# A DLRM tower on one core: hot ids laid out once per partition, a later load of the other ids, and another order of work

## The chip, the cores and the metric

The kernel runs on one core of one Trainium2 chip. The metric is the device time of one execution in microseconds (us); lower is better. PE is TensorE, DVE is VectorE, ACT is ScalarE, POOL is GpSimd, SP is SyncE, which only issues DMAs here.

## The reference

```python
e = jnp.stack([tbl_0[ids[:, 0]], ..., tbl_31[ids[:, 31]]], axis=1)     # 512 x 32 x 64, f32
idx_i, idx_j = np.triu_indices(32, k=1)                                # 496 pairs of fields
left = jnp.einsum('bpd,pde->bpe', e[:, idx_i, :], W)                   # W: 496 x 64 x 64
z = jnp.sum(left * e[:, idx_j, :], axis=-1)                            # 512 x 496
h = jnp.concatenate([z, dense_ctx], axis=1)                            # 512 x 512
h = jnp.maximum(h @ W_top1 + b_top1, 0.0)                              # 512 wide
h = jnp.maximum(h @ W_top2 + b_top2, 0.0)                              # 256 wide
y = h @ W_top3                                                         # 512 x 1
```

The tables have 1,000 to 125,000 rows of 64 numbers. Everything is f32.

## The kernel before, in words

The batch of 512 is worked in four quarters of 128 rows, one row per partition. The 32 fields form 16 units of two fields. The 496 pairs form 31 groups of 16; a group is named by the units it moves (`moving(g)`, the left factors) and the units it multiplies with (`others(g)`). Group 0 holds the pairs inside units. W stays in SBUF, one 256 KB load for each group, and serves all four quarters.

For each quarter and group:
- PE multiplies the transposed embeddings `xt` with W into one of three PSUM slots (`LEFT_BUFS`), 1024 columns wide;
- DVE multiplies the slot with the other factor (a product);
- the product is summed over 64 numbers in one of four ways, the last letter of the word in `ORDER`: A by ACT (`add_rows`, 16 accumulating instructions, a ring of four buffers), D by a DVE reduction (`sum_rows`), P by POOL (`add_halves`, six halvings, a ring of two buffers), C by PE (the group is computed transposed, `col_group`, and summed by matmuls with a selector, `reduce`).

A, D and P read the other factor from the gathered rows, C from their transpose.

The rows come in two ways. The 24 large or middle tables, and all fields in quarters 1 to 3, are gathered by 120 indirect DMAs of POOL (`fetch`, L396), one for each field and quarter. Eight small tables ("hot", units 12 to 15) are, for the first quarter only, loaded whole by SP (8 loads of 256 KB, `load_hot`, L336), and looked up by matmul: DVE compares the ids with row numbers (`compare`, L515, 16 instructions in two sets), PE multiplies the tables with these 0/1 matrices (`look_up`, L675, words `h0` and `h1`). For that the ids of the four fields of a set must stand in every partition: `load_ids` (L342) reads one row of 4 x 128 ids from DRAM to all 128 partitions.

Gathered units are transposed by PE and copied to `xt` by ACT or DVE (`turn`, a word like `0t6-9a`: quarter 0, units 6 to 9, the copy by ACT where it ends in `a`).

The order of all this is written out by hand as words in `ORDER` (L51): `0g8` is a gather of unit 8 in quarter 0, `o0.1` a half set of compares, `0:21A` the matmul and product of group 21, `0=21` its sum, `f`, `z` the folding of the sums into z, `l1.0`, `m1`, `n1` the three dense layers of a span of columns. Each engine walks the list and does what is its own, strictly in that order, and waits on semaphores for the rest. All the engines' orders follow from this one list, and so does the order of the W loads (`W_ORDER`, the order of quarter 0's groups).

SP's queue (L346 on): ids of quarter 0, hot ids of set 0, four tables, hot ids of set 1, W loads number 0 and 1, four tables, the ids of the three later quarters (L355), then W loads 2 to 30. Loads 2 to 7 go in pairs, each pair behind the landing of a unit that quarter 0 gathers: the first two to be complete in `GATHERED` and so on (L358). From number 8 (`W_AHEAD`) a load waits for the product of the group eight places before it. POOL waits for the later ids only before its first gather of quarter 1 (L421).

Of the kernel before, what the change touches and what calls it, by code (L numbers as in the profile page):

```python
# [211 lines left out]
def build(nc, a):  # L212
    ctx = ExitStack()
    with ctx:
# [118 lines left out]
        def _(sp):  # L333
# [8 lines left out]
            def load_ids(d):  # L342
                sp.dma_start(hot_ids[d], a["hot_ids"][4 * d:4 * d + 4, :].unsqueeze(0).to_broadcast([P, 4, PB])
                             ).then_inc(hot_ids_loaded[d], 16)
# [4 lines left out]
            for d in range(1, HOT_SETS):  # L349
                load_ids(d)  # L350
                load_w(W_ORDER[d - 1])
                if d == HOT_SETS - 1:
                    load_w(W_ORDER[d])
# [565 lines left out]
```

## Time and profile before

| | us |
|---|---|
| median of 3 runs | 200.62 (200.47 to 201.2) |
| the profiled execution | 200.62 |
| its span (first to last instruction) | 198.5 |
| outside the span | 2.12 |
| DVE / ACT / PE / POOL busy | 181.4 / 173.5 / 190.0 / 144.5 |
| granted TensorE clock | 1.0 in every slice |

A busy PE is not PE at its peak: matmuls are pipelined, and their ends are modelled. Instructions of DVE overlap a little, too, so the cost of one in a row of many is the distance from start to start, not its duration. A row of the timeline gives the start, the time until the last of the merged instructions ends, the engine, line, operation and tiles, the count, and in brackets the idle time before it with what ended it.

### The profile page before, as it was taken

To read this page: it belongs to the slowest core of one execution; us is meant where nothing else is said; L and a number is where in the kernel's file an instruction comes from. 1 tells how busy PE (TensorE), PEld (TensorE's weight loads), DVE (VectorE), ACT (ScalarE), POOL (GpSimd) and SP (SyncE) were. 2 spreads that over 40 slices of the span, in tenths; PEclk is the share of its full clock that TensorE was granted. 3 is DMA by queue.
4 is the path that set the end of the run, shared out by engine and by line. 5 is a ranking of instruction groups with operands and counts; after the bars stand their busy time and mean duration, and the time that the engine had idled before them with its cause. 6 is when DMAs were issued, how large, how long until landed. Compare 5 with 4: busy or idle time off the path is not lost.

```text
span 198.5 us, 7004 instructions
## 1 busy us (share of the span) xinstructions
PE 190.0 (96%) x2340; PEld 155.3 (78%) x2340; DVE 181.4 (91%) x196; ACT 173.5 (87%) x1587; POOL 144.5 (73%) x181
## 2 busy tenths in 40 slices
PE   6968899999999999999999999999999999999994
PEld 6856778789678777978778877987866789868983
DVE  2663999999999999999999999999999999999952
ACT  6001999999999998999999999999999999999920
POOL 5787777777777777777777777777787885898620
PEclk9999999999999999999999999999999999999999
DMA  3996778887481111111111111111110100000000
GB/s 96 362 346 215 201 184 253 252 253 227 116 314 26 31 25 28 28 30 28 30 26 31 28 26 31 26 31 26 29 22 16 27 3 3 0 5 2 3 0 0
DMA packets 11099, 16.80 MB, mean 85 GB/s; under 512 B 3624, under 2 KB 3624, under 8 KB 10936
## 3 DMA queue, kind: packets, MB, share of 16 engines
q1 hardware_dynamic: 7224, 12.43, 19.1%
q0 software_dynamic: 3840, 3.94, 10.1%
q8 instruction: 18, 0.29, 0.7%
q14 instruction: 17, 0.14, 0.3%
HBM read 16.36 MB, written 0.00 MB: 82 GB/s over the span
## 4 chain that ended last, share of the span: by engine, by line
PE 49%; ACT 16%; DVE 16%; issue 9%; DMA 4%; POOL 4%; DVEq 0%; ACTq 0%
PE left L714 21%; ACT prod_act L442 15%; PE left L724 9%; PE zsum L737 6%; DVE prod_act L566 5%; DVE prod_col L586 4%; POOL rows L396 4%; PE left L797 4%; DMA rows<-tbl_dram,ids 3%; DVE prod_dve L566 2%; PE left L787 2%; PE left L703 2%; DVE sums L611 2%; PE zsum L745 2%; PE left L692 1%
## 5 line engine op out<-in xcount | busy, mean ns | idle before, releaser
L442 ACT ACTIVATE prod_act<-prod_act 128x64 f32<-128x64 f32 x784 | 162.8, 602 | 0.3 <-DVE prod_act L566 0.3
L442 ACT ACTIVATION_READ_ACCUMULATOR prod_act<-prod_act 128x1 f32 x784 | 161.1, 515 | 0.0
L396 POOL DMA_INDIRECT rows<-tbl_dram,ids x120 | 114.6, 955 | 37.7 <-issue 34.3
L714 PE MATMUL left<-w,xt 64*128 64x256 f32 x584 | 73.5, 387 | 1.0 <-DVE prod_col L586 0.7
L714 PEld LDWEIGHTS left<-w,xt 64*128 64x128 f32 x584 | 52.4, 187 | 14.2 <-issue 5.4
L566 DVE TENSOR_TENSOR prod_act<-left,rows 128x1024 f32<-128x1024 f32 x45 | 53.8, 1215 | 1.6 <-DMA rows<-tbl_dram,ids 1.4
L724 PEld LDWEIGHTS left<-xt,w 64*128 64x128 f32 x752 | 45.2, 188 | 4.3 <-issue 2.1
L724 PE MATMUL left<-xt,w 64*128 64x128 f32 x752 | 48.2, 276 | 0.0
L586 DVE TENSOR_TENSOR prod_col<-left,xt 128x1024 f32<-128x1024 f32 x39 | 46.1, 1214 | 0.2 <-PE left L724 0.2
L409 POOL TENSOR_TENSOR prod_pool<-prod_pool 128x512 f32<-128x512 f32 (+4 forms) x45 | 27.4, 609 | 6.4 <-DVE prod_pool L566 3.5
L737 PE MATMUL zsum<-prod_col,selector 128*32 128x256 f32 x376 | 25.0, 385 | 0.1
L566 DVE TENSOR_TENSOR prod_dve<-left,rows 128x1024 f32<-128x1024 f32 x19 | 23.0, 1216 | 0.3 <-PE left L714 0.2
L611 DVE TENSOR_REDUCE sums<-prod_dve 128x16 f32<-128x1024 f32 x19 | 22.9, 1207 | 0.0
L737 PEld LDWEIGHTS zsum<-prod_col,selector 128*32 128x32 f32 x376 | 9.9, 109 | 9.7 <-issue 2.3
L479 ACT ACTIVATE xt<-left 128x1024 f32<-128x1024 f32 (+3 forms) x8 | 8.6, 1076 | 8.3 <-PE left L692 8.3
L787 PE MATMUL left<-z,w 128*128 128x256 f32 (+1 forms) x64 | 11.8, 335 | 0.0
L787 PEld LDWEIGHTS left<-z,w 128*128 128x128 f32 x64 | 9.8, 190 | 1.9 <-DVE prod_dve L566 0.7
L566 DVE TENSOR_TENSOR prod_pool<-left,rows 128x1024 f32<-128x1024 f32 x9 | 10.9, 1213 | 0.0
L515 DVE TENSOR_SCALAR prod_col<-prod_act,row_cast 128x512 f32<-128x512 int32 x16 | 6.8, 496 | 3.7 <-DMA prod_act<-hot_ids_dram 3.7
L583 DVE TENSOR_TENSOR prod_col<-left,xt 128x1024 f32<-128x1024 f32 x8 | 9.7, 1216 | 0.1
L675 PE MATMUL left<-prod_col,w 128*64 128x128 f32 x96 | 5.9, 277 | 2.2 <-DMA w<-tbl_dram 2.2
L703 PE MATMUL left<-w,xt 64*128 64x64 f32 x128 | 7.7, 271 | 0.0
(48 smaller groups left out, 100.1 us busy)
## 6 DMA issues: line engine op xcount, KB each, us to landing
w<-pair_w_dram SPq DMA_DIRECT2D x31, 256.0 KB, 3.4
rows<-tbl_dram,ids POOLq DMA_INDIRECT x120, 2.5
w<-tbl_dram SPq DMA_DIRECT2D x6, 256.0 KB, 4.9
w<-w_top_dram SPq DMA_DIRECT2D x1, 1024.0 KB
prod_act<-hot_ids_dram SPq DMA_DIRECT2D x2, 256.0 KB, 5.3
h<-tbl_dram SPq DMA_DIRECT2D x2, 256.0 KB, 7.0
w<-w_top_dram SPq DMA_DIRECT2D x1, 512.0 KB
z<-dense_t_dram SPq DMA_DIRECT2D x16, 2.0 KB
```

The source lines that it names most:

```text
L396: pool.indirect_dma_start(out=rows[:, part % ROW_BUFS, n, h, :], out_offset=None, in_=a[f"tbl_{f}"], in_offset=bass.IndirectOffsetOnAxis(a ...
L409: pool.tensor_tensor(prod[:, :, :half], prod[:, :, :half], prod[:, :, half:2 * half], ALU.add).then_inc(pool_halved, 1)
L442: op = act.activation(p, p, ACT.Copy, accum_out=act_sums[:, k:k + 1])
L566: dve.tensor_tensor(out.rearrange("p (j e) d -> p j (e d)", j=4), slot(item).rearrange("p (j e) -> p j e", j=4), other.unsqueeze(1).to_bro ...
L583: dve.tensor_tensor(out, slot(item).rearrange("p (h u b) -> p h u b", h=2, b=PB), other, ALU.mult).then_inc(dve_taken, 1)
L586: dve.tensor_tensor(out.rearrange("p h (j m) b -> p (h j) (m b)", j=2), slot(item).rearrange("p (j e) -> p j e", j=4), other, ALU.mult).th ...
L611: dve.tensor_reduce(sums_of(part, g), prod.rearrange("p (h u o) d -> p h u o d", h=2, o=2), AXIS.X, ALU.add).then_inc(dve_summed, 1)
L703: mm = pe.matmul(slot(item)[:, col:col + D], xt[own, part % 2, 2 * k + half, :], w[own, INSIDE, :, :].rearrange("p u c -> p (u c)")[:, D * ...
L714: mm = pe.matmul(slot(item)[:, col:col + P * per], xt[own, part % 2, GROUPS[g][i][0], :], w[own, g, i:i + per, :], start=True, stop=True)
L724: mm = pe.matmul(slot(item)[:, col:col + PB], w[own, g, i, :], xt[own, part % 2, n, :], start=True, stop=True)
L737: mm = pe.matmul(zsums(pair)[32 * s:32 * s + 32, :], selector[:, 30 - 2 * q:62 - 2 * q], prod_col[:, (COL_FROM + c) % COL_BUFS, half, odd: ...
L787: mm = pe.matmul(slot(item)[:, :n], w1[:, c, P * k:P * k + P], z[:, c, SPANS[i]], start=(c == 0), stop=(c == NZ - 1))
```

## The change

It has four parts.
- The hot ids stand in DRAM as 2 x 128 x 4 x 128 numbers, each partition's copy in its own 2 KB; `load_ids` reads them straight instead of one row 128 times.
- In SP's queue W load 1 comes after the second four tables instead of before them, and the later quarters' ids are loaded behind W loads 0 to 7 instead of ahead of W load 2.
- `ORDER` and `ACT_GROUPS` are new. Sums by way and quarter: A 12, 12, 14, 11 become 11, 12, 12, 12; C 15, 16, 9, 7 become 16, 16, 13, 3; D 4, 3, 7, 5 become 4, 3, 6, 7; P 0, 0, 1, 8 become 0, 0, 0, 9. `W_ORDER` and the order of the gathers follow.
- The rows of z are placed by another rule (`FIRST`), which changes which row of W_top1 stands where and no instruction count: each quarter folds four chunks before and after.

```diff
 ORDER = [
-    "0g8 0g9 0g8 0g9 0g7 o0.0 o0.1 0g6 0g6 h0a 0g7 o1.0 0g11 0g11 o1.1 0g10 h1 0g10 0:21A 0g1 0t6-9a 0g0 0:27D 0g0",
-    "0:12A 0:22C 0=21 u 0g1 0=27 0t10-11a 0:30A 0:23C 0=12 0:28C 0=30 0g5 0g3 0:24A 0g4 0=23 0=22 0t0-1 0:2C 0:29C",
...
-    "3=4 n0 3=10 3=14 3=7 3:5A 3=11 3:19A 3:22P l1.0 l1.2 e v 3=9 l1.1 3=5 3=22 3:15D 3=16 3:12P 3:26D 3=19 l1.3",
-    "3=15 3=26 3=12 m1a d f3 z3 n1 l2.0 l2.1 l2.2 l2.3 m2a n2",
+    "o0.0 0g9 0g8 o0.1 0g10 o1.0 o1.1 h0 0g10 0g9 0g11 0g8 h1a 0g11 0g4 0:22A 0g6 0g4 0g6 0g5 0:30C 0t8-11a 0:29C",
+    "0=22 0:23A 0g5 0:2C 0:17C 0=29 0g7 0:11A 0g7 0g3 0g2 0:28C 0:20A 0=23 0=11 0g1 0:21A 0=17 0g2 0=30 0g1 0t6-7",
+    "0:15A 0g3 0=20 0g0 0:12C 0g0 0:27C 1g11 1g15 0:16C 1g13 0=28 0:8A 1g14 1g12 0=21 0:10D 1g13 0:19A u 1g14 1g15",
...
+    "2:24A 3g6 3g1 2:25D 2=24 3g1 3:28P 3g5 2=14 2=25 2=7 2=12 2=13 2=5 2=10 3:22A 3:29P 3g5 3:23A 3t7-11a f2 3g2",
+    "3g4 3g3 z2 3=22 3:17D 3:21A 3g4 3g3 3:24A 3:18A 3=23 3=17 l0.3a 3t0-1a 3g2 3=21 3:30C 3:20A 3:13D 3:12D 3=30",
+    "3t2-6a 3:9A 3=28 3=24 3:7P 3:16C 3:19A 3=18 3=19 3=29 3:27C 3=7 3:0P 3=20 3=0 3:6A 3:5P 3=12 3=13 3:26D m0a 3=5",
+    "3:14P 3:3D 3:10P 3:11A n0 3=6 3=14 3=10 3=3 3=9 3=27 3=16 l1.0 l1.1a 3=26 3:8A 3:2P 3:15A l1.2 e v 3=11 3:1P",
+    "3:4D 3:25D 3=8 3=2 3=4 3=15 l1.3 d 3=1 3=25 m1a f3 z3 n1 l2.0a l2.1a l2.2a l2.3a m2a n2",
 ]
-ACT_GROUPS = [30, 18, 24, 19, 11, 16, 0, 5, 13, 21, 20, 12, 15, 9]
+ACT_GROUPS = [15, 19, 24, 11, 18, 22, 9, 8, 20, 23, 21, 6]
...
-FIRST += [g for g in range(NG) if g not in FIRST and WAY[LAST, g] != "C"][:16 - len(FIRST)]
+MORE = [g for g in range(NG) if g not in FIRST and WAY[LAST, g] != "C"]
+FIRST += sorted(MORE, key=lambda g: [WAY[part, g] for part in range(LAST)].count("C"))[:16 - len(FIRST)]
...
             def load_ids(d):
-                sp.dma_start(hot_ids[d], a["hot_ids"][4 * d:4 * d + 4, :].unsqueeze(0).to_broadcast([P, 4, PB])
-                             ).then_inc(hot_ids_loaded[d], 16)
+                sp.dma_start(hot_ids[d], a["hot_ids"][d]).then_inc(hot_ids_loaded[d], 16)
...
             for d in range(1, HOT_SETS):
                 load_ids(d)
                 load_w(W_ORDER[d - 1])
-                if d == HOT_SETS - 1:
-                    load_w(W_ORDER[d])
                 load_hot(d)
-            sp.dma_start(ids[:, 1:, :], a["ids"][P:, :].rearrange("(t p) f -> p t f", p=P)).then_inc(later_ids_loaded, 16)
+            load_w(W_ORDER[HOT_SETS - 1])
             for k in range(W_FIRST, NG):
+                if k == W_AHEAD:
+                    sp.dma_start(ids[:, 1:, :], a["ids"][P:, :].rearrange("(t p) f -> p t f", p=P)).then_inc(later_ids_loaded, 16)
                 if k < W_AHEAD:
                     sp.wait_ge(*rows_there(0, GATHERED[(k - 2) // 2]))
...
-    arrays["hot_ids"] = arrays["ids"][:PB, HOT_FIELDS].T
+    hot_ids = arrays["ids"][:PB, HOT_FIELDS].T.reshape(HOT_SETS, 1, 4, PB)
+    arrays["hot_ids"] = np.broadcast_to(hot_ids, (HOT_SETS, P, 4, PB))
```

The copy of the first look-up goes from ACT to DVE and that of the second from DVE to ACT. Of the dense layers, the words `l0.2a`, `l0.3a`, `l1.1a`, `m0a` and the four `l2` words now end in `a`: ACT does that work (for `m0a` half of it), which DVE did before.

## Rows read from the trace of the kernel before

**Rows 1.** The page, part 1: busy us, share of the span, instructions.

```profile
PE 190.0 (96%) x2340; PEld 155.3 (78%) x2340; DVE 181.4 (91%) x196; ACT 173.5 (87%) x1587; POOL 144.5 (73%) x181
```

**Rows 2.** Windows: stretch, length, busy of PE, PEld, DVE, ACT, POOL, clock, DMA, GB/s.

```profile
0.00:18.70 18.70, 14.32 (x164) 12.99 (x165) 8.56 (x22) 3.67 (x4) 13.30 (x19) 1.00 0.76 249
18.70:190.30 171.60, 170.47 (x2110) 137.64 (x2110) 170.56 (x166) 169.49 (x1582) 131.24 (x163) 1.00 0.27 71
```

**Rows 3.** Timeline of DVE, a dense stretch.

```profile
63.89 0.41 DVE L526 COPY xt<-left 128x256 f32<-128x256 f32 x1
64.22 3.47 DVE L586 TENSOR_TENSOR prod_col<-left,xt 128x1024 f32<-128x1024 f32 x3
67.62 1.21 DVE L566 TENSOR_TENSOR prod_act<-left,rows 128x1024 f32<-128x1024 f32 x1
```

**Rows 4.** Timeline of DVE, the first 31 us.

```profile
9.87 3.46 DVE L515 TENSOR_SCALAR prod_col<-prod_act,row_cast 128x512 f32<-128x512 int32 x8 [0.82 <-DMA prod_act<-hot_ids_dram]
...
18.72 1.23 DVE L566 TENSOR_TENSOR prod_act<-left,rows 128x1024 f32<-128x1024 f32 x1 [1.40 <-DMA rows<-tbl_dram,ids]
...
30.78 1.22 DVE L586 TENSOR_TENSOR prod_col<-left,xt 128x1024 f32<-128x1024 f32 x1
```

**Rows 5.** The chain that ended last, in order of time: start, us, what.

```profile
12.57 6.03 DMA rows<-tbl_dram,ids
```

**Rows 6.** Timeline of PE, 7 to 20 us.

```profile
13.13 1.97 PE L675 MATMUL left<-prod_col,w 128*64 128x128 f32 x32 [1.85 <-DMA w<-tbl_dram]
14.93 1.92 PE L675 MATMUL left<-prod_col,h 128*64 128x128 f32 x32
16.78 1.13 PE L714 MATMUL left<-w,xt 64*128 64x256 f32 x8
...
18.64 0.40 PE L692 MATMUL left<-ident,rows 64*128 64x64 f32 x6 [0.68 <-DMA rows<-tbl_dram,ids]
```

**Rows 7.** Timeline of POOL: the first gathers, the last one, the last partial sums.

```profile
2.83 1.10 POOL L396 DMA_INDIRECT rows<-tbl_dram,ids  x1 [1.26 <-DMA ids<-ids_dram]
4.23 0.94 POOL L396 DMA_INDIRECT rows<-tbl_dram,ids  x1 [0.30 <-issue]
...
156.58 0.94 POOL L396 DMA_INDIRECT rows<-tbl_dram,ids  x1 [0.30 <-issue]
...
186.45 3.35 POOL L409 TENSOR_TENSOR prod_pool<-prod_pool 128x512 f32<-128x512 f32 x5 [1.28 <-DVE prod_pool L566]
189.88 0.22 POOL L415 TENSOR_TENSOR sums<-prod_pool 128x16 f32<-128x16 f32 x1
```

**Rows 8.** Timeline of SP's queue, W loads 6 and 7.

```profile
17.17 0.81 SPq L340 DMA_DIRECT2D w<-pair_w_dram  x2
```

**Rows 9.** The gather issued at 20.3 us, and how long until it landed.

```profile
L396 POOL DMA_INDIRECT rows<-tbl_dram,ids x1: 945/945/945, 20.3 to 20.3; - x1
DMA to landing us min/median/max: 3.6/3.6/3.6
```

**Rows 10.** Windows, columns as in rows 2: the DMA engines early on.

```profile
3.00:4.00 1.00, 1.00 (x6) 1.00 (x6) 0.00 (x0) 1.00 (x1) 0.93 (x1) 1.00 0.62 104
4.00:5.00 1.00, 1.00 (x7) 1.00 (x6) 0.00 (x0) 0.04 (x1) 0.77 (x1) 1.00 0.83 244
5.00:6.00 1.00, 1.00 (x7) 1.00 (x7) 0.32 (x1) 0.00 (x0) 0.69 (x2) 1.00 1.01 371
6.00:16.00 10.00, 7.82 (x121) 7.01 (x122) 6.51 (x16) 0.39 (x1) 7.86 (x8) 1.00 1.02 355
```

**Rows 11.** Groups of instructions, shapes apart: busy, mean ns, idle before.

```profile
L442 ACT ACTIVATE prod_act<-prod_act 128x64 f32<-128x64 f32 x784 | 162.8, 602 | 0.3 <-DVE prod_act L566 0.3
L592 DVE TENSOR_SCALAR h<-left,b 128x256 f32<-128x256 f32 x4 | 1.9, 470 | 0.0
L592 DVE TENSOR_SCALAR h<-left,b 128x128 f32<-128x128 f32 x8 | 2.5, 343 | 1.4 <-PE left L781 1.4
```

**Rows 12.** Waits: engine, line, waited for: us in total, times, longest.

```profile
POOL prod_pool L409 <- DVE prod_pool L566: 3.5, 3, 1.9
```

26 rows, old and new, of the table ORDER are left out of this document.

## The prediction, made before the changed kernel was run

> **What bounds the kernel now.** I read the busy times first, then the windows, then DVE's timeline, then the chain. PE shows the highest busy share, but its ends are modelled [rows 1]. The windows say more: from 18.70 to 190.30 us DVE is busy 170.56 of 171.60 us, so it stands idle for 1.0 us in all; ACT is busy 169.49 [rows 2]. Before 18.70 DVE is busy for only 8.56 us. The span is therefore DVE's list of work, packed end to end, with a start of 18.7 us ahead of it and a tail of 8.2 us behind it. In the packed stretch a 1024-wide operation costs 1.13 us from start to start (three of them in 67.62 - 64.22 = 3.40), a 256-wide copy 0.33 [rows 3]. DVE has 124 products and 19 reductions: 143 x 1.13 = 161.6 of the 170.6 us. So only three things can move the time: when DVE starts, how much it has to do, and the holes in between.
>
> What ends the start? The first product, at 18.72, waited 1.40 us for gathered rows [rows 4], and the chain names the gather issued at 12.57, which landed 6.03 us later, at 18.60 [rows 5]. Counting POOL's gathers, that is the eighth, and group 21 reads unit 7, which the eighth completes. Just under this wait lies another: the second look-up waited on PE until 13.13 for its tables, then ran without a pause to 16.78, and the matmul of group 21 behind it took 1.13 to 17.91 [rows 6]. Rows and tables are within 0.7 us of each other, so both must improve.
>
> **The rows at the start.** In the new list the first product is group 22, which reads units 8 and 9. The new gather order is 9, 8, 10, 10, 9, 11, 8, 11, ..., so both are there with the seventh gather. In the old list the seventh gather completed unit 6, and SP's wait on it ended at 17.17, when it issued W loads 6 and 7 [rows 8]. POOL's pace is one gather in 1.25 us from 2.83 on (4.23 after the first, 0.94 plus 0.30 of issue) [rows 7], and the change doesn't touch it. So the rows would be there at 17.2 at the latest under the same traffic. They could come earlier: the seventh is issued at 11.0 and a later one takes 3.6 us [rows 9], which would give 14.6. I take 17.0, near the row of the same gather.
>
> What could make them earlier is less DMA work in the way, for the engines are full from 5 to 16 us (share 1.02) [rows 10]. The landings of early gathers take 6 us and of later ones 3.6, so here they do suffer from SP's loads. The Trainium skill (DMA: Bandwidth & Descriptors, Queues, rings and completion order) says that each DMA engine takes turns between the queues it has work for, a packet at a time, so that a long backlog on SP's queue would not hold up a gather. By that rule alone the seventh gather would land at 17.2 as before and the first product come at 17.3, 0.2 us later than I take it.
>
> **The look-up at the start.** Two things bring the tables forward. W load 1 (256 KB) no longer stands before the second four tables: at 371 GB/s [rows 10] that is 0.7 us. And the first read of hot ids may be quicker: between 3 and 5 us the engines are 0.62 and 0.83 busy but move only 104 and 244 GB/s, where 371 GB/s go with 1.01 later [rows 10]. At that rate 348 GB/s would need 0.95 us of busy time, not 1.45, so 0.5 us of engine time goes to slow packets while the same 2 KB is read 128 times. Whether that is the repeated read or a cold start the trace doesn't tell: bounds 0 and 0.5 from this row, and 1.5 if the idle part of these two microseconds went too. I take 0.4, since the slow packets fall together with this load. The look-up chain then gives 17.91 - 0.7 - 0.4 = 16.8. The second compares end at 9.87 + 3.46 = 13.33 [rows 4], and PE needs one more half look-up (1.9) and the matmul (1.1) behind them: 16.4, no bound. That DVE now copies the first look-up (0.4) behind all 16 compares, at 13.3, delays nobody: units 12 and 13 are not moved before 15.
>
> So the first product comes at 17.1 (bounds 16.4 and 17.5), 1.6 us earlier. What is late next? The third product (29C) needs units 10 and 11 turned, and that turn needs the eighth gather, which landed at 18.60. From there PE's turn is 0.4 and ACT's copy 0.6 us: 19.7. Two products lie ahead of it, so DVE's list can't run as if it had started before 19.7 - 2 x 1.13 = 17.4; PE's matmul of 29 stands behind that turn too and would give 17.7. If the eighth gather comes 1 us earlier both give 16.7 or less. The seventh product (11A) needs the fourteenth gather, issued at 20.3 and landed 3.6 later [rows 9]: 23.9 - 6 x 1.13 = 17.1. These are starts of an unbroken list, so the old one must be put in the same terms: at 30.78 [rows 4] ten wide operations and one 256-wide copy lie behind it, 30.78 - 10 x 1.13 - 0.33 = 19.15. I take 17.5 for the new one, bounds 16.8 and 18.5: gain 1.65 us, 0.65 to 2.35.
>
> **DVE's list.** 20 reductions instead of 19: +1.13. Layer 1 of span 0 gives two of four copies to ACT and layer 2 one of two: 256 wide, 470 ns each [rows 11], about 0.39 from start to start like the other narrow ones, -1.17. Layer 1 of span 1 gives one: 128 wide, 343 ns, 0.26. Turn copies: 256, 512, 256 and 256 columns become 256, 512 and 512 (0.33 and 0.60), -0.06. Sum -0.36. The four copies that go to ACT in the tail are 343 ns and PE's matmuls are still going when the first are done; ACT stood idle there, and I cost this at 0 (0 to +0.2).
>
> **The other engines.** ACT loses two sums of 162.8 / 49 = 3.3 us each [rows 11], gains 12 turns instead of 8 (+0.8 to +1.2) and four small copies (1.6): about -4, and it begins sooner with the first product. POOL has the same 120 gathers and nine sums. PE swaps a row group for a column group and its selector matmuls (+0.45) in a stretch that it has slack in. None of them becomes shorter than DVE's list, so none of it counts, except as cover.
>
> **The later ids and the W loads.** POOL needs the later ids before gather 25, at 2.83 + 24 x 1.25 = 33. They go out after W load 7, behind 17.2; even with 7 us to land they are there at 25. W loads 2 and 3 now wait for the fourth gather instead of the third, 1.3 us later, with load 2 needed third. It would be there around 18, when PE comes to it behind the turn. Cost 0, and 0.5 if not; this is in the 18.5 above. Queued behind these waits on SP is nothing but more W.
>
> **The holes.** Before, DVE idled 1.0 us after 18.7. The new order has several points early on where rows arrive within half a microsecond of DVE's need (11A, 20A, the turn of units 0 to 5 ahead of 26C). I add 0.4 us (bounds -0.7, all holes but 0.3 closed, and +2).
>
> **Sum.** -1.65 - 0.36 + 0.4 = -1.6. Span 198.5 - 1.6 = 196.9; with the 2.12 us around it 199.0, against the profiled execution's own 200.62, which is also the median. Its own range is 198.2 to 199.6.
>
> **The rivals.**
> - The start gets better still and ACT's slack closes holes: start 16.8 (-2.35), list -0.36, holes -0.7: 197.2. For it: the DMA engines are full while the start waits. Against: POOL's pace. Chance 0.1.
> - The gain dies on POOL's pace. DVE is ready sooner, but rows come one gather in 1.25 us as before, and W loads 2 to 7 and the later ids now fall into 13 to 20 us. If the fourteenth gather takes 5 us instead of 3.6, as the early ones do, the list starts at 25.3 - 6.8 = 18.5: -0.65 - 0.36 + 0.4 = -0.6, 200.0. Chance 0.24.
> - Slower: POOL's nine sums all crowd into the last quarter. Two buffers, 3.62 us a sum. POOL's gathers end earlier (2.83 + 120 x 1.25 = 152.8 instead of 157.5), so back to back the sums end at 152.8 + 9 x 3.62 = 185.4, and DVE's list at 190.3 - 1.65 - 0.36 = 188.3. In the old kernel POOL's last sum ended at 190.10 [rows 7] and DVE's list at 190.3 [rows 2], so POOL is already nearly last. If it idles for products by more than 188.3 - 185.4 = 2.9 us the end goes with it; the old one idled 3.5 over three sums [rows 12]. Twice those 3.5 gives 192.4, 2.3 later than before: 202.9. PE waits for it in the last fold, and layer 2 of span 0 (16 matmuls of 256) also moved into this stretch. Against it: the new list puts two P products before the gathers are over. Chance 0.14.
> - The repeated read was not slow at all (0 instead of 0.4): the look-up gives 17.2, under the 17.5 of the turn. It stays within the forecast.
>
> **How the numbers follow.** Forecast 0.52, all of it faster by over 0.5% (1.0 us, under 199.6; about what a measurement of this kernel can tell from no change). Faster: 0.52 + 0.10 + 0.03 = 0.65. Same: most of the second rival, 0.21. Slower: 0.14. The range goes from 197.6, which leaves out half of the first rival, to 201.2, which leaves out most of the slower one.
>
> **What would show it.** Right: first product near 17.1; DVE's tenth wide operation 1.6 us earlier; hot ids landed before 5.4; the second look-up starting near 12.0; DVE idle about 1.4 us from there on; the end (last fold) at 189. The slower rival shows as POOL idle before L409 and the last fold released by POOL. Wrong altogether: if DVE's holes after 31 us grow beyond 2 us, for then the order and not the start decides.

## The result, and the profile after

The changed kernel took 199.34 us (median of 4 runs, 199.07 to 199.53), the kernel before beside it 200.61 (4 runs, 200.47 to 201.2): a ratio of 0.993 with a 95% interval of 0.9907 to 0.9953, 1.3 us faster. The forecast was 199.0 in a range of 197.6 to 201.2. The profiled execution of after took 199.53 us, its span 197.4, against 200.62 and 198.5. The granted clock was 1.0 in every slice of both. In some executions it was 0.99 over the whole span and the time longer: of the 27 of the kernel before that are used first below, six took 201.5 to 201.7 us, and the median of the other 21 is 200.26.

The busy times of after, to be held against [rows 1]: DVE has 1.6 us less, ACT 3.1 less, POOL the same.

```profile
PE 189.4 (96%) x2380; PEld 156.6 (79%) x2380; DVE 179.8 (91%) x188; ACT 170.4 (86%) x1535; POOL 144.7 (73%) x181
```

Windows of after, from the first product to the last fold of z (columns as in [rows 2]). Look at length against DVE's busy time, the third of the busy numbers.

```profile
16.18:31.00 14.82, 13.72 (x188) 10.87 (x186) 13.45 (x13) 12.39 (x118) 11.15 (x13) 1.00 0.86 257
31.00:60.00 29.00, 28.08 (x399) 21.93 (x396) 28.33 (x26) 27.76 (x252) 21.99 (x24) 1.00 0.70 211
60.00:100.00 40.00, 39.95 (x562) 32.35 (x564) 39.70 (x38) 38.85 (x380) 30.25 (x33) 1.00 0.14 28
100.00:150.00 50.00, 50.00 (x616) 41.53 (x614) 50.00 (x49) 47.23 (x434) 37.81 (x41) 1.00 0.14 29
150.00:189.10 39.10, 39.10 (x401) 32.65 (x398) 38.65 (x39) 38.48 (x359) 32.12 (x58) 1.00 0.03 6
```

DVE starts its list 2.54 us earlier than before (16.18 instead of 18.72), and then stands idle for 1.37 us before 31, for 0.67 between 31 and 60 and for 0.75 after that, 2.8 in all; before, it was 1.0 us from 18.70 on [rows 2]. So 1.8 of the 2.54 us are given back in waits, most of them before 60 us. DVE's timeline has the places (compare [rows 4]).

```profile
3.99 3.26 DVE L515 TENSOR_SCALAR prod_col<-prod_act,row_cast 128x512 f32<-128x512 int32 x8 [1.15 <-DMA prod_act<-hot_ids_dram]
8.95 3.26 DVE L515 TENSOR_SCALAR prod_col<-prod_act,row_cast 128x512 f32<-128x512 int32 x8 [1.70 <-DMA prod_act<-hot_ids_dram]
...
16.18 1.22 DVE L566 TENSOR_TENSOR prod_act<-left,rows 128x1024 f32<-128x1024 f32 x1 [3.64 <-PE left L714]
...
24.52 1.23 DVE L566 TENSOR_TENSOR prod_act<-left,rows 128x1024 f32<-128x1024 f32 x1 [1.24 <-DMA rows<-tbl_dram,ids]
...
29.39 1.21 DVE L566 TENSOR_TENSOR prod_act<-left,rows 128x1024 f32<-128x1024 f32 x1
...
56.23 1.22 DVE L566 TENSOR_TENSOR prod_act<-left,rows 128x1024 f32<-128x1024 f32 x1 [0.53 <-DMA rows<-tbl_dram,ids]
...
60.87 1.22 DVE L611 TENSOR_REDUCE sums<-prod_dve 128x16 f32<-128x1024 f32 x1
```

The first product no longer waits for rows but for PE, that is, for the look-up. PE's timeline (compare [rows 6]):

```profile
6.84 3.71 PE L675 MATMUL left<-prod_col,w 128*64 128x128 f32 x64 [0.63 <-DMA w<-tbl_dram]
11.35 1.97 PE L675 MATMUL left<-prod_col,w 128*64 128x128 f32 x32 [0.80 <-DMA w<-tbl_dram]
13.15 1.92 PE L675 MATMUL left<-prod_col,h 128*64 128x128 f32 x32
14.99 1.13 PE L714 MATMUL left<-w,xt 64*128 64x256 f32 x8
15.96 1.06 PE L724 MATMUL left<-xt,w 64*128 64x128 f32 x16
16.85 0.41 PE L692 MATMUL left<-ident,rows 64*128 64x64 f32 x8
```

**The balance.** Ten wide operations and a narrow copy lie ahead of 29.39, as they did ahead of 30.78 before: 1.39 us gained by there (2.54 at the start, 1.15 lost again). The copy that ends z starts at 189.92 instead of 191.07, 1.15 gained. So between the two places the list takes 160.53 us instead of 160.29, although it has 0.36 us less to do by the prediction's count: 0.60 us of new waits. Behind the copy come 7.48 us instead of 7.43. That is -1.39 - 0.36 + 0.60 + 0.05 = -1.1, the difference of the spans.

### The profile page after: what moved, and what is told of

Read it like the earlier page. It is cut to its first block, busy times and chain, and to the rows that moved or that the text cites. A ratio compares the mean times of both kernels' runs of the same rounds, so it can differ in the third digit from the quotient of the medians.

```text
span 197.4 us, 7040 instructions
## 1 busy us (share of the span) xinstructions
PE 189.4 (96%) x2380; PEld 156.6 (79%) x2380; DVE 179.8 (91%) x188; ACT 170.4 (86%) x1535; POOL 144.7 (73%) x181
## 4 chain that ended last, share of the span: by engine, by line
PE 66%; POOL 18%; issue 7%; DMA 4%; DVE 3%; ACT 0%; DVEq 0%; ACTq 0%; POOLq 0%
PE left L714 26%; POOL rows L396 18%; PE left L724 14%; PE zsum L737 8%; PE left L787 6%; PE left L797 4%; DMA rows<-tbl_dram,ids 3%; PE left L703 3%; PE left L692 2%; PE zsum L745 1%; DVE prod_act L566 1%; PE left L781 1%; PE left L772 1%; DMA ids<-ids_dram 1%; DVE sums L611 1%
## 5 line engine op out<-in xcount | busy, mean ns | idle before, releaser
L442 ACT ACTIVATE prod_act<-prod_act 128x64 f32<-128x64 f32 x752 | 157.7, 588 | 2.5 <-DVE prod_act L566 2.5
L442 ACT ACTIVATION_READ_ACCUMULATOR prod_act<-prod_act 128x1 f32 x752 | 155.5, 501 | 0.0
L714 PE MATMUL left<-w,xt 64*128 64x256 f32 (+1 forms) x600 | 72.0, 378 | 1.0 <-DVE prod_act L566 0.9
L566 DVE TENSOR_TENSOR prod_act<-left,rows 128x1024 f32<-128x1024 f32 x47 | 56.3, 1213 | 5.5 <-PE left L714 3.6
L586 DVE TENSOR_TENSOR prod_col<-left,xt 128x1024 f32<-128x1024 f32 x43 | 50.7, 1214 | 0.7 <-PE left L724 0.2
L724 PEld LDWEIGHTS left<-xt,w 64*128 64x128 f32 x768 | 46.5, 188 | 3.5 <-DVE prod_act L566 1.1
L566 DVE TENSOR_TENSOR prod_dve<-left,rows 128x1024 f32<-128x1024 f32 x16 | 19.2, 1213 | 0.1
L479 ACT ACTIVATE xt<-left 128x512 f32<-128x512 f32 (+5 forms) x12 | 9.1, 771 | 5.7 <-PE left L692 5.7
L471 ACT ACTIVATE xt<-left 128x256 f32<-128x256 f32 x1 | 0.4, 385 | 11.1 <-PE left L675 11.1
L692 PEld LDWEIGHTS left<-ident,rows 64*128 64x128 f32 x120 | 5.2, 138 | 4.5 <-issue 2.3
L797 PE MATMUL left<-h,w 128*128 128x128 f32 (+1 forms) x48 | 7.6, 312 | 0.0
```

The source lines that it names most:

```text
L442: op = act.activation(p, p, ACT.Copy, accum_out=act_sums[:, k:k + 1])
L566: dve.tensor_tensor(out.rearrange("p (j e) d -> p j (e d)", j=4), slot(item).rearrange("p (j e) -> p j e", j=4), other.unsqueeze(1).to_bro ...
L586: dve.tensor_tensor(out.rearrange("p h (j m) b -> p (h j) (m b)", j=2), slot(item).rearrange("p (j e) -> p j e", j=4), other, ALU.mult).th ...
L714: mm = pe.matmul(slot(item)[:, col:col + P * per], xt[own, part % 2, GROUPS[g][i][0], :], w[own, g, i:i + per, :], start=True, stop=True)
L724: mm = pe.matmul(slot(item)[:, col:col + PB], w[own, g, i, :], xt[own, part % 2, n, :], start=True, stop=True)
L797: mm = pe.matmul(slot(item)[:, BANK * o:BANK * o + n], w2[:, k, P * o:P * o + P], h1[:, k, :n], start=(k == 0), stop=(k == H1 // P - 1))
```

## The experiments

The first four take the change apart. The kernel before beside them took 200.52 us (27 runs).

**The layout alone.**

```diff
-                sp.dma_start(hot_ids[d], a["hot_ids"][4 * d:4 * d + 4, :].unsqueeze(0).to_broadcast([P, 4, PB])
-                             ).then_inc(hot_ids_loaded[d], 16)
+                sp.dma_start(hot_ids[d], a["hot_ids"][d]).then_inc(hot_ids_loaded[d], 16)
...
```

> The kernel before with nothing but the new layout of the hot ids. Theory (two chains set the start, rows and look-up, and the old order's first product waits for its eighth gather): the hot ids of set 0 land near 3.9 us instead of 5.6, the look-ups run earlier, but the first product still comes at 18.0 to 18.7, and the time changes by 0 to -0.5 us. Rival (the layout is the whole gain): first product 1.5 us earlier or more, time -1.2 us.

Measured: 200.02 us (10 runs), ratio 0.9976 (0.995 to 1.0002), which no change would also give; the profiled execution took 201.0. DVE's timeline of it:

```profile
3.99 3.26 DVE L514 TENSOR_SCALAR prod_col<-prod_act,row_cast 128x512 f32<-128x512 int32 x8 [1.16 <-DMA prod_act<-hot_ids_dram]
8.48 3.27 DVE L514 TENSOR_SCALAR prod_col<-prod_act,row_cast 128x512 f32<-128x512 int32 x8 [1.23 <-DMA prod_act<-hot_ids_dram]
15.16 0.42 DVE L519 COPY xt<-left 128x256 f32<-128x256 f32 x1 [3.42 <-PE left L674]
17.35 1.22 DVE L565 TENSOR_TENSOR prod_act<-left,rows 128x1024 f32<-128x1024 f32 x1 [1.76 <-DMA rows<-tbl_dram,ids]
...
60.26 3.49 DVE L565 TENSOR_TENSOR prod_act<-left,rows 128x1024 f32<-128x1024 f32 x3 [0.80 <-DMA rows<-tbl_dram,ids]
```

The compares start at 3.99, the first product at 17.35, 1.37 earlier than in [rows 4] and earlier than I had expected (18.0 to 18.7): the eighth gather was issued at 13.03 and landed 4.2 us later, where it took 6.03 before. But the three products at 60.26 started at 59.84 in the kernel before: the early start is lost, and in this execution more than that, in three waits of 0.3 to 0.8 us, two for rows and one for PE. The second look-up starts at 11.40, where it was 13.13 [rows 6].

**SP's queue alone.** The order of W load 1 and of the later ids as in the change, the old layout and the old `ORDER`.

> The kernel before with nothing but the new order of SP's queue (W load 1 behind the second tables, the later ids behind W load 7). Theory: 0.7 us less ahead of the second tables, so the second look-up starts near 12.4 instead of 13.1; the rows of the eighth gather land 0 to 0.8 us earlier; first product 17.8 to 18.7, time -0.1 to -0.8 us. Rival (by queue turns a backlog on SP's queue does not hold up gathers): rows land at 18.6 as before, time unchanged.

Measured: 200.09 us (10 runs), ratio 0.9959 (0.9936 to 0.9981). The hot ids land at 5.46 (5.58 before), the second look-up starts at 12.13, 1.00 earlier, the first product at 18.14, 0.58 earlier, the products of 59.84 at 59.35, 0.5 us earlier, with no new wait of note.

**Both, with the old order.** 

> The kernel before with the layout and SP's queue order, and its own order of work. Theory: look-up chain down by 2 us as in the changed kernel, so rows alone decide: first product when the eighth gather lands, 17 to 18; and as this order had no holes of size behind the start, what the start gains stays: time -0.7 to -1.5 us, near the changed kernel's -1.3. Rival (the new order is needed for the gain): under -0.5 us.

Measured: 199.96 us (10 runs), ratio 0.9965 (0.9936 to 0.9994). The first product starts at 16.41, 2.31 earlier than before; the products of 59.84 start at 59.01, 0.83 earlier. Lost in between are 0.68 us on PE, 0.17 and 0.56 on rows. I had expected 0.7 to 1.5 us and that what the start gains stays; it was 0.6, and two thirds of the start's gain went into waits. The second look-up starts at 11.44, no earlier than with the layout alone.

**The order alone**, old layout and old queue. 

> The changed kernel with the old layout of the hot ids and the old order of SP's queue: the new order of work alone. Theory: the look-up chain stands as before, so the first product comes at 17.9 (look-up 16.8 and one matmul), 1.8 us later than in the changed kernel; the hole before group 11 (rows of the fourteenth gather) shrinks from 1.3 us to nothing in return, so the time is only 0.3 to 0.8 us above the changed kernel, -0.5 to -1.0 us against the kernel before. Rival (the new order costs, layout and queue pay for it): slower than before by 0.5 us or more.

Measured: 199.61 us (6 runs), ratio 0.9942 (0.9922 to 0.9961). The first product starts at 18.05, 0.67 earlier than before (it needs seven gathers, not eight, and waits for the look-up) and 1.87 later than in the whole change; yet the time is within 0.3 us of that, as expected. Two rows of DVE's timeline show why.

```profile
18.05 1.23 DVE L567 TENSOR_TENSOR prod_act<-left,rows 128x1024 f32<-128x1024 f32 x1 [4.45 <-PE left L715]
...
61.05 1.22 DVE L612 TENSOR_REDUCE sums<-prod_dve 128x16 f32<-128x1024 f32 x1
```

The reduction that after starts at 60.87 starts here at 61.05. The start differs from after's by 1.87 us, this place by 0.18. The wait for the fourteenth gather, 1.24 us in after, is 0.16 here.

So an earlier start than this one's is nearly all lost before 61 us. What takes it? Theory B: POOL's gathers, one in 1.25 us [rows 7]. Theory A: single collisions that can be moved, the load of the dense layers' weights above all, which falls on the gathers just ahead of 56 us. The chain of after, and its windows of that stretch (against 90 and 303 GB/s in 52 to 56 before):

```profile
50.45 5.66 DMA rows<-tbl_dram,ids
```

```profile
50.00:52.00 2.00, 2.00 (x42) 1.59 (x36) 2.00 (x3) 2.00 (x22) 1.39 (x3) 1.00 0.52 77
52.00:54.00 2.00, 2.00 (x28) 1.69 (x26) 2.00 (x3) 2.00 (x26) 1.59 (x2) 1.00 0.69 262
54.00:56.00 2.00, 2.00 (x34) 1.13 (x35) 1.70 (x2) 2.00 (x27) 1.50 (x2) 1.00 0.97 398
```

The kernel before beside the next four took 200.50 us (26 runs).

**The dense layers' weights later**, behind the twelfth product of quarter 1.

```diff
+MLP_AFTER = [at for at in MAINS if at[0] == 1][11]
...
+            for t in taken(ITEM[MLP_AFTER]):
+                sp.wait_ge(*t)
```

> The changed kernel, with the five loads of the dense layers' weights (1.5 MB) held back until the twelfth product of quarter 1 (some 17 us later). Theory (these loads now collide with the gather that the first product of quarter 1 waits for: issued at 50.45 us, landed 5.66 later): that gather lands in 2.5 to 3 us, the hole of 0.53 at 56.2 us goes, time -0.3 to -0.6 us against the changed kernel. Rival (POOL's pace alone makes the holes): the hole stays, time unchanged.

Measured: 199.53 us (12 runs), ratio 0.9953 (0.9928 to 0.9978). The gather of this place (50.23) now lands in 2.3 us and the hole at 56 is gone, but in this execution the seventh product waited 2.14 us, till 25.24, for the gather issued at 20.3, which took 4.9 us. That is ahead of everything this edit touches, so it is scatter of the gather's landing, not a hole that moved. The reduction comes at 60.97. By the 12 runs there is no gain over after either.

**The gathers in another order**, so that units are complete when they are needed first; groups 15 and 21 exchanged.

```diff
-    "o0.0 0g9 0g8 o0.1 0g10 o1.0 o1.1 h0 0g10 0g9 0g11 0g8 h1a 0g11 0g4 0:22A 0g6 0g4 0g6 0g5 0:30C 0t8-11a 0:29C",
-    "0=22 0:23A 0g5 0:2C 0:17C 0=29 0g7 0:11A 0g7 0g3 0g2 0:28C 0:20A 0=23 0=11 0g1 0:21A 0=17 0g2 0=30 0g1 0t6-7",
+    "o0.0 0g9 0g8 o0.1 0g10 o1.0 o1.1 h0 0g10 0g9 0g11 0g8 h1a 0g11 0g4 0:22A 0g4 0g5 0g5 0g6 0:30C 0t8-11a 0:29C",
+    "0=22 0:23A 0g6 0:2C 0:17C 0=29 0g7 0:11A 0g7 0g3 0g2 0:28C 0:20A 0=23 0=11 0g1 0:15A 0=17 0g2 0=30 0g1 0t6-7",
...
```

> The changed kernel with the gathers of quarter 0 in the order 4, 4, 5, 5, 6, 6, 7, 7 instead of 4, 6, 4, 6, 5, 5, 7, 7, and groups 21 and 15 exchanged in the list. Group 11 then needs the twelfth gather instead of the fourteenth. Theory A (a local misorder): the hole of 1.24 us at 24.5 goes and stays gone, time -1.0 to -1.3 us against the changed kernel. Theory B (POOL's pace): the hole at 24.5 goes, but DVE then waits for the turn of units 0 to 5 behind the twenty-fourth gather, at about 38 us, so that at 40 us it is where it was, give or take 0.2, and the time changes by 0 to -0.3 us.

Measured: 199.69 us (12 runs), ratio 0.9951 (0.993 to 0.9973). DVE waits 0.78 us at 23.88 and 0.70 at 38.57 for PE and 1.03 at 56.65 for rows; the reduction comes at 61.30. The wait at 38.57 is the one that theory B names: PE turns units 0 to 5 as soon as the rows of the twenty-fourth gather (issued at 33.05) are there. Here is this turn in PE's timeline of after and of this run:

```profile
36.93 0.58 PE L692 MATMUL left<-ident,rows 64*128 64x64 f32 x12 [0.84 <-DMA rows<-tbl_dram,ids]
```

```profile
36.99 0.59 PE L692 MATMUL left<-ident,rows 64*128 64x64 f32 x12 [1.55 <-DMA rows<-tbl_dram,ids]
```

The product behind it starts at 38.65 in after and at 38.57 here, though the hole at 24.5 is a third smaller. Both edits together gave the same time:

> Both edits of the two runs before (weights of the dense layers later, gathers in the order 4, 4, 5, 5, 6, 6, 7, 7). Theory B: the sum of both, -0.3 to -0.9 us against the changed kernel, 198.4 to 199.0 us; with theory A of the gather order it would be -1.5 us.

Measured: 199.48 us (9 runs), ratio 0.9949 (0.9929 to 0.997). The waits for rows at 24 and at 56 are gone, one of 1.30 us for PE stands at 38.65, the same place again, with 0.45 behind it, and the reduction comes at 60.98. My step that removing both holes would bring 0.3 to 0.9 us was wrong: the wait moved to the product behind the turn of units 0 to 5.

**Two gathers less**, the run that tells POOL's pace from single collisions. It leaves out the two gathers of unit 10 in quarter 0; SP loads the first 128 rows of these two tables instead, which are not the rows of the ids.

```diff
+PLAIN = 10
...
+            for h in (0, 1):
+                sp.dma_start(rows[:, 0, PLAIN, h, :], a[f"tbl_{FIELDS[2 * PLAIN + h]}"][:P, :]).then_inc(plain_loaded, 16)
...
+                if (part, n) == (0, PLAIN):
+                    return
```

> The changed kernel, with the two gathers of unit 10 in quarter 0 taken from POOL; SP loads the first 128 rows of those two tables instead (so unit 10 of quarter 0 has other rows than the reference's). Every later gather comes 2.5 us earlier. Theory B (POOL's pace makes the holes): the first product stays at 16.2, for the look-up sets it; the holes at 24.5, 38.6 and 56.2 go; time -1.2 to -2.2 us against the changed kernel. Rival (the matmuls or the DMA traffic make the holes): -0.5 us or less.

Measured: 197.14 us (4 runs), ratio 0.9827 (0.9796 to 0.9859), 2.2 us under the kernel after by the medians, 1.8 by the profiled executions (197.76 and 199.53). DVE's timeline has no wait left between these two rows:

```profile
16.49 1.23 DVE L574 TENSOR_TENSOR prod_act<-left,rows 128x1024 f32<-128x1024 f32 x1 [3.58 <-PE left L722]
...
59.24 1.22 DVE L619 TENSOR_REDUCE sums<-prod_dve 128x16 f32<-128x1024 f32 x1
```

It starts 0.31 us later than after and comes to the same reduction 1.63 us earlier: 42.75 us from the one to the other instead of 44.69. The order of the work is the same in both, so the 1.94 us between them is waiting, and it goes when each later gather comes 2.5 us (two steps of 1.25) earlier. The chain that ended last says the same. Its shares by engine in after, here, and in the second run of the sixteen copies further down:

```profile
PE 66%; POOL 18%; issue 7%; DMA 4%; DVE 3%; ACT 0%; DVEq 0%; ACTq 0%; POOLq 0%
```

```profile
PE 85%; DVE 5%; DMA 3%; issue 2%; SPq 2%; ACT 0%; DVEq 0%; ACTq 0%
```

```profile
PE 85%; DVE 8%; DMA 3%; issue 2%; SPq 1%; ACT 0%; DVEq 0%; ACTq 0%
```

In after the chain runs from gather to gather up to the one of 50.45, and only then on to DVE. In the other two no gather is on it: it starts with the loads of the tables.

**More cover for DVE.** Two tries to put work that is ready ahead of the places where DVE waits: 0:24A ahead of the turn of units 0 to 5, a reduction and 1:30D ahead of 1:22A; once on top of both edits, once with after's order of gathers and the weights later (this diff).

```diff
-    "1g10 0=10 1g12 0t0-5a 1g9 0:26C 0:6C 0=19 1g8 0:4C 1g8 1g9 1g10 0=15 0:13C 0:0D 0:9A 0=8 1g11 0:1C 1g0 0=2",
-    "0:24A 1g1 0:3C 0:7D 0:18A 0=27 0=0 1g0 0=24 1g3 0=13 0=3 1t12-15a 0:25C 0:14C 0:5D 1:22A 0=18 0=7 1g2 0=12 0=1",
-    "0=26 1g1 0=9 0=5 0=25 0=4 0=6 1:30D 1t8-8a 1g2 1g4 1g3 1t9-11a 0=16 2g15 1g6 0=14 1g5 1g5 1=30 1=22 f0 1g7 z0",
+    "1g10 0=10 1g12 0:24A 0t0-5a 1g9 0:26C 0:6C 0=19 1g8 0:4C 1g8 1g9 1g10 0=15 0:13C 0:0D 0:9A 0=8 1g11 0:1C 1g0 0=2",
+    "1g1 0:3C 0:7D 0:18A 0=27 0=0 1g0 0=24 1g3 0=13 0=3 1t12-15a 0:25C 0:14C 0:5D 0=7 1:30D 0=18 1g2 0=12 0=1",
+    "0=26 1g1 0=9 0=5 0=25 0=4 0=6 1:22A 1t8-8a 1g2 1g4 1g3 1t9-11a 0=16 2g15 1g6 0=14 1g5 1g5 1=30 1=22 f0 1g7 z0",
...
```

> The run with both edits (dense weights later, gathers 4, 4, 5, 5, 6, 6, 7, 7), and two more moves in the list: group 24 of quarter 0 ahead of the turn of units 0 to 5 (it needs the gathered rows of units 0 and 1, not their transpose, so it can fill DVE's wait for that turn), and in quarter 1 group 30 and a reduction ahead of group 22 (group 30 reads units 12 and 13, already turned, so the rows of units 8 and 9 are needed 2.3 us later). Theory B (POOL's pace is the bound in quarter 0, and only work that does not need new rows can cover it): the hole of 1.4 us at 38.6 us shrinks to 0.3, the one at 56 us is gone, -0.8 to -1.4 us against the run with both edits, 198.1 to 198.8 us. Rival (DVE is then stopped by ACT's ring or PE): no gain.

> The same moves and the later dense weights on the changed kernel's own gather order. Theory B: the hole at 24.5 us (1.3) stays, the later ones go: -0.5 to -1.0 us against the changed kernel, 198.3 to 198.9 us, near the run before. Rival as there: no gain.

Measured, beside a kernel before of 200.54 us (17 runs): 199.52 us (7 runs, 0.9946, 0.9933 to 0.9958) and 199.99 us (12 runs, one of them 203.84; 0.9978, 0.9954 to 1.0002). No gain in either, and the second looks slower than after (0.9978 against 0.993). In the first there is no wait left at 38.6, but one of 1.34 us for PE at 19.41 and one of 0.87 us at 82.96 (a turn); in the second one of 1.71 us for rows stands at 25.25. The waits at 19.41 and 25.25 lie ahead of the words that were moved, so the moves did not cause them; why the covered holes bring nothing over the many runs is open.

**Sixteen copies instead of 128**, each read by eight partitions. This asks how many copies the quicker read needs.

```diff
-                sp.dma_start(hot_ids[d], a["hot_ids"][d]).then_inc(hot_ids_loaded[d], 16)
+                sp.dma_start(hot_ids[d], a["hot_ids"][d].unsqueeze(1).to_broadcast([16, 8, 4, PB])
+                             ).then_inc(hot_ids_loaded[d], 16)
...
-    arrays["hot_ids"] = np.broadcast_to(hot_ids, (HOT_SETS, P, 4, PB))
+    arrays["hot_ids"] = np.broadcast_to(hot_ids, (HOT_SETS, 16, 4, PB))
```

> The changed kernel with 16 copies of the hot ids in DRAM instead of 128, each read by 8 partitions. If it is the many reads of one 2 KB place that made the first load of hot ids land at 5.58 us instead of 3.88, eight reads of each of 16 places should land in between, nearer to the 128 copies: 3.9 to 4.5 us, and the first compare starts at 4.0 to 4.6 us. If it is the size of the place in DRAM or a cold start, the old 5.6 us stays.

Measured: 198.76 us (one run); the first hot ids land at 4.74, midway between 3.88 and 5.58 and a little later than expected, the first compare starts at 4.84, the first product at 16.79, the reduction at 60.22. This is a single time, below all of after's; the same kernel in more runs:

> The kernel after with 16 copies of the hot ids in place of 128, each copy read by 8 partitions, now timed in rounds (its one look gave 198.76 us with the hot ids landed at 4.74 us). Theory A (GpSimd's gathers set the first 60 us, and what starts earlier waits later): within 0.3% of the kernel after, 199.2 to 199.8 us, the product near 61 us at its place within 0.3 us. Theory B (the later compares keep out of the way of GpSimd's gathers or of W's load, and the gain is real): 198.6 to 199.0 us, the product near 61 us at least 0.5 us earlier than in the kernel after.

Measured: 199.44 us (6 runs, 198.82 to 199.64), ratio 0.9933 (0.9914 to 0.9952) against before's 200.61: the same as after. Its profiled execution is, by chance, a test of what a late start costs. The tables landed late (two loads at 8.3 and 10.0 us, the second hot ids at 11.1), PE rested 2.00 us ahead of 8.30, and the granted clock was 0.88 on average from 5 to 10 us and 0.78 from 10 to 15 (1.0 is 2.4 GHz), where after had 1.0 throughout. The first product started 2.11 us later than after's. DVE's timeline:

```profile
18.29 1.23 DVE L567 TENSOR_TENSOR prod_act<-left,rows 128x1024 f32<-128x1024 f32 x1 [3.34 <-PE left L715]
...
61.04 1.22 DVE L612 TENSOR_REDUCE sums<-prod_dve 128x16 f32<-128x1024 f32 x1
```

2.11 us later at the start, 0.17 us later here, 0.19 us at the copy of z. This list has no wait between the two rows: 61.04 is its own start plus 42.75 us of work. So it shows that a start as late as 18.3 costs next to nothing, as after's earlier start goes into waits; that both come out so near 61 is in part luck.

**All together.** Six of these kernels, and after, have the same DVE work between the first product and this reduction. From the reduction to the copy of z they all take the same, 129.03 to 129.07 us but for one (129.39).

| kernel | first product | reduction | between | copy of z | median |
|---|---|---|---|---|---|
| after | 16.18 | 60.87 | 44.69 | 189.92 | 199.34 |
| order alone | 18.05 | 61.05 | 43.00 | 190.12 | 199.61 |
| weights later | 15.99 | 60.97 | 44.98 | 190.03 | 199.53 |
| gathers reordered | 15.99 | 61.30 | 45.31 | 190.36 | 199.69 |
| both edits | 15.81 | 60.98 | 45.17 | 190.37 | 199.48 |
| sixteen copies, first | 16.79 | 60.22 | 43.43 | 189.25 | 198.76 |
| sixteen copies, second | 18.29 | 61.04 | 42.75 | 190.11 | 199.44 |
| two gathers less | 16.49 | 59.24 | 42.75 | 188.29 | 197.14 |

With 120 gathers the reduction comes between 60.2 and 61.3, whether the list starts at 15.8 or at 18.3; with two gathers taken away it comes at 59.24 and the list is as dense as that which started at 18.29. What is shown is that the number of gathers ahead of a unit sets the time of the lists that start before 18, with how long the single gather takes to land as the scatter on it. Which gather's landing stops which product differs from execution to execution. POOL itself was not equally early in all: its fourteenth gather was issued at 20.43 in after and at 19.98 in the first run of the sixteen copies, so 0.45 of the 0.65 us by which that one reached the reduction earlier are POOL's own. In the five lists with 120 gathers that start before 17 the reduction comes 40.2 to 40.7 us behind this gather. Why POOL was earlier there (its first gather 0.16 us, the rest from fewer slow gathers beside the compares, see the end) and not in the repeat (20.33) is not shown.

## Why the prediction was right, and where its steps missed

**The first product: right side, mis-sized.** 17.1 was forecast with bounds of 16.4 and 17.5; 16.18 came, below both. The look-up chain was rightly its bound in the new list, but one term of it was too small: the slow read of the hot ids. I took 0.4 us of bounds 0, 0.5 and 1.5. It was more than the widest of them. The first set landed at 5.58 before and at 3.88 in after, 1.70 us, with the second set 0.92 (9.85 and 8.92). The minima below are the first set's. SP's group L343 of before:

```profile
DMA to landing us min/median/max: 4.4/5.3/6.3
```

The same group, L344, of after:

```profile
DMA to landing us min/median/max: 2.7/4.0/5.4
```

The windows of [rows 10] had the sign: the stretch that moved 104 GB/s there moves 375 in after.

```profile
3.00:4.00 1.00, 1.00 (x6) 1.00 (x6) 0.01 (x1) 1.00 (x1) 0.89 (x1) 1.00 1.07 375
```

The failed step is that I counted only the slow packets' busy time, when the idle share of those two microseconds went as well: the bound of 1.5 that I had written down and left. W load 1 behind the tables was taken at 0.7. The two don't add up as I added them: by the start of the second look-up the queue alone gave 13.13 - 12.13 = 1.00, the layout alone 13.13 - 11.40 = 1.73, and both together 1.69 in the old order and 1.78 in after. With the new layout the queue's part brings the look-up nothing more.

**The second look-up**: 12.0 forecast, 11.35 measured, for the same reason: 1.78 us earlier, where 0.7 + 0.4 = 1.1 was put down.

**The list's start: near.** I had put 17.5 for it (the old one 19.15), after's is 29.39 - 10 x 1.13 - 0.33 = 17.76. The prediction named what would hold it: the seventh product (11A) needs the fourteenth gather. I had it landing at 23.9. It was issued at 20.43 and landed 4.0 us later instead of 3.6; DVE waited for it till 24.52. That this wait and not the first product sets the start is why the 0.9 us that the first product came earlier than forecast brought nothing. The place behind the tenth wide operation comes 1.39 us earlier; 1.6 was forecast. The gather's rows:

```profile
L396 POOL DMA_INDIRECT rows<-tbl_dram,ids x1: 947/947/947, 20.4 to 20.4; - x1
...
who waited for it (us, times):
  DVE prod_act L566: 1.2, 1
```

**The rows at the start: mis-sized too, without effect.** I had the seventh gather landing at 17.0. After's was issued at 11.44 and landed 3.0 us later, at 14.4, near the 14.6 that I had given as the early end; the turn of units 8 to 11 then ran at 16.85 without waiting for the eighth, which in before landed at 18.60. The gather's group in after:

```profile
L396 POOL DMA_INDIRECT rows<-tbl_dram,ids x1: 1184/1184/1184, 11.4 to 11.4; - x1
...
DMA to landing us min/median/max: 3.0/3.0/3.0
```

The DMA engines' share from 10 to 15 us was 0.69 in after and 1.03 in the same five microseconds before (1.02 from 6 to 16 [rows 10]), and the gather landed in half the time of before's eighth, 3.0 us for 6.03. The Trainium skill (DMA: Bandwidth & Descriptors, Queues, rings and completion order) had been read as no gain here, since the engines take turns between queues; in these traces the gathers land later where the engines are busier (3.0 us at a share of 0.69, 6.03 at 1.03), whatever the cause.

**DVE's list, the tail, the later ids, the W loads.** DVE has 188 instructions instead of 196 and 1.6 us less busy time. The prediction's count gives +1.13 for the reduction, -1.17 - 0.26 - 0.06 in the list and -4 x 0.34 in the tail, -1.7. The tail is 0.05 us longer. POOL didn't wait for the later ids (issued at 15.66; the first gather that needs them started at 34.19), and among the waits of after there is none of note for a W load.

**The holes: mis-sized.** 0.4 us was put down with bounds of -0.7 and 2; it was 0.60 behind the tenth wide operation, most of it the wait at 56.23. I had looked for holes in the first 40 us and had not seen that the new order asks for quarter 1's units sooner, so that the gather of 50.45 had to land while SP loads the dense layers' weights. "DVE idle about 1.4 us from there on" holds if it is counted from 31 on, as the wait for the fourteenth gather is in the list's start: 1.4 us from 31 to 189.10 by the windows. From the first product on it is 2.8.

**The rival on POOL's pace** was put at 200.0 and 0.24. Its time was wrong, but its mechanism was at work: POOL's gathers hold the first 60 us. Two executions even had the very landing that it assumed, the fourteenth gather 4.9 and 5.0 us behind its issue: with the weights later the list's start was 25.24 - 6.78 = 18.46, with the order alone 25.31 - 6.78 = 18.53, and the rival had 18.5. They took 199.55 and 199.64 us, not 200.0, as behind that place they had next to no waits. The forecast with after's measured start of the list (17.76 instead of 17.5) is 199.3; that this is the median is in part luck, for the holes and the tail came out 0.25 us dearer, and by the profiled executions the gain is 1.1 us, not 1.6. The rival with a better start (197.2) came in no run with all the gathers (the lowest single time is 198.76); with two of them taken away it was 197.1.

**The slower rival** did not come. POOL waited for products for 1.9 us in two of its nine sums, and 2.9 was its point of decision. POOL's timeline at the end (compare [rows 7]):

```profile
181.36 3.35 POOL L409 TENSOR_TENSOR prod_pool<-prod_pool 128x512 f32<-128x512 f32 x5 [1.03 <-DVE prod_pool L560]
184.79 0.22 POOL L415 TENSOR_TENSOR sums<-prod_pool 128x16 f32<-128x16 f32 x1
184.97 3.35 POOL L409 TENSOR_TENSOR prod_pool<-prod_pool 128x512 f32<-128x512 f32 x5
188.40 0.22 POOL L415 TENSOR_TENSOR sums<-prod_pool 128x16 f32<-128x16 f32 x1
```

Its last sum ends at 188.62, the last reduction of DVE just behind it (187.88 + 1.2), and PE's last fold starts at 189.27 without a wait: 0.6 us to spare. The fold was forecast for 189.

**Which part brings the gain.** The prediction put 1.65 us on the earlier start and 0.36 on the list. By the medians the new order alone, with the old layout and queue, brings 0.9 of the 1.3 us (200.52 - 199.61). In the old order the layout brings 0.5, the queue 0.4 and both together 0.6; in the new order both bring some 0.3, which lies inside the intervals. Against 200.26, the median of before's runs at the full clock, the order brings 0.65, the layout 0.24, the queue 0.17 and these two together 0.3. So how much layout and queue bring in the new order is open: 0.3 us by 199.61 - 199.34, 0.6 if the order's 0.65 is taken from the whole 1.3. In both countings the order alone is the largest single part: the direction was right while the weight was on the wrong part. In DVE's terms the order alone gives 0.67 at the start and 0.36 of work, with no new waits: 43.00 us to the reduction, against 42.75 in the densest of the lists.

## What to carry to other kernels

When a dense engine starts earlier, look for the producer whose pace doesn't change, and work out for each of the consumer's places in the first stretch when its input can be there at the earliest: the latest of these, taken back to the start, is the gain, and not the start itself. Then test it by taking two of the producer's steps away; reordering gained nothing here (four orders, 199.5 to 200.0 us). A wait in one profiled execution that lies ahead of the edit is scatter and says nothing about the edit. A read of one small row by all partitions is worth laying out as copies when it stands at the head of the program, but only what the producer's pace leaves of it is gained.

## What the runs showed that I had not expected

- The read of the same 2 KB by 128 partitions took 4.4 us to land as the program's second DMA (4.3 to 4.7 in three kernels), the same bytes from 128 places 2.7 us (2.5 to 3.3 in nine), from 16 places, each read by eight partitions, 3.6 us (3.5 in the repeat). A cold start would be the same in all of them, so it isn't what made the old read slow. Its issue on SP took 0.69 us with the 16 copies and 0.41 with the 128.
- The gather's pace is not constant. It takes 0.94 us where DVE is idle or multiplies, and up to 1.28 where it runs beside DVE's compares (int32 to f32, 512 wide). POOL's timeline of after:

```profile
4.20 1.19 POOL L396 DMA_INDIRECT rows<-tbl_dram,ids  x1 [0.31 <-issue]
5.69 1.28 POOL L396 DMA_INDIRECT rows<-tbl_dram,ids  x1 [0.30 <-issue]
7.27 0.94 POOL L396 DMA_INDIRECT rows<-tbl_dram,ids  x1 [0.30 <-issue]
8.52 1.03 POOL L396 DMA_INDIRECT rows<-tbl_dram,ids  x1 [0.30 <-issue]
9.85 1.28 POOL L396 DMA_INDIRECT rows<-tbl_dram,ids  x1 [0.30 <-issue]
11.44 1.18 POOL L396 DMA_INDIRECT rows<-tbl_dram,ids  x1 [0.30 <-issue]
12.93 0.94 POOL L396 DMA_INDIRECT rows<-tbl_dram,ids  x1 [0.30 <-issue]
```

  The compares lie at 3.99 to 7.25 and 8.95 to 12.21. The five slow ones add 1.26 us over 0.94 each; before had four, which add 1.09. Why a gather is slower there is not shown, and whether compares elsewhere would give this microsecond back wasn't tried.
- The landing of one and the same gather, the fourteenth at 20.3 to 20.4 us, took 3.6 us in before, 4.0 in after and 4.9 with the weights later. The one at 50.4 us took 5.66 us beside the load of the dense weights and 2.3 without it. Two profiled executions of kernels that differ by little can so differ by 0.7 us in the first 60 us.
